# First layer norm of a fused attention and FFN block: normalisation on ScalarE, weight and bias in the transposed eviction and on GpSimd

## The reference, cut to what matters

```python
xn = layernorm(x)                                # no weight, no bias
# branch 1: attention block on xn
attn = softmax(scores(xn)) @ v                   # 16 heads of 16, causal, 512 x 512 scores a head
y = xn + (ctx @ out_w + out_b)
h = (y - mean(y)) / sqrt(var(y) + 1e-5) * ln1_g + ln1_b     # the first layer norm
f = gelu(h @ ffn_w1 + ffn_b1) @ ffn_w2 + ffn_b2             # 256 -> 1024 -> 256
s = layernorm(h + f) * ln2_g + ln2_b
# branch 2: gated FFN on xn with blockwise FP4 rounding of activations and weights
g = silu(ffn_ref(xn))                            # 256 -> 2 x 704 -> 256
out = x + s * g
```

## Time and profile before

| | us |
|---|---|
| median of 3 runs | 1925.8 (1923.6 to 1926.86) |
| the profiled execution, its own time | 1926.66 |
| its span, first to last instruction | 1924.9 |
| TensorE matmul busy | 1821.6 (95%) |
| VectorE busy | 1597.8 (83%) |
| GpSimd busy | 1165.4 (61%) |
| ScalarE busy | 950.6 (49%) |

### The profile page before, as it was taken

One profiled execution on the slowest core, in us unless ns is written; L12 is line 12 of the kernel. 1 busy time (PEld: TensorE's weight loads), 2 busy tenths in 40 slices (PEclk: granted clock), 3 DMA queues, 4 the chain that ended last, 5 costly groups with the idle time before them and its releaser, 6 DMA issues.

```text
span 1924.9 us, 37358 instructions
## 1 busy us (share of the span) xinstructions
PE 1821.6 (95%) x12693; PEld 1308.1 (68%) x12693; DVE 1597.8 (83%) x5143; ACT 950.6 (49%) x1940; POOL 1165.4 (61%) x825
## 2 busy tenths in 40 slices
PE   8886999999999999999999999999999999999997
PEld 3333667676776767677776767677776767777766
DVE  5888878888898978888897988888897888889763
ACT  3543545453635545463645545463554545364542
POOL 1434856575765757575775757586675657576472
PEclk8988999999999999999999999999999999999999
DMA  5532233333323333332323333331433333332211
GB/s 151 161 105 79 75 97 109 87 108 87 101 63 108 109 97 92 96 116 64 113 75 97 109 101 94 97 107 53 122 90 97 110 86 109 83 98 71 64 56 34
DMA packets 146647, 181.44 MB, mean 94 GB/s; under 512 B 20461, under 2 KB 101486, under 8 KB 146452
## 3 DMA queue, kind: packets, MB, share of 16 engines
...
...
## 4 chain that ended last, share of the span: by engine, by line
PE 67%; DVE 18%; issue 7%; POOL 3%; ACT 2%; DMA 2%; SPq 0%; POOLq 0%; ACTq 0%; DVEq 0%
PE ps L765 12%; PE ps L774 11%; PE ps L706 10%; PE ps L723 5%; PE ps L629 4%; PE ps L679 4%; PE ps L663 3%; PE ps L616 3%; PE ps L738 3%; PE ps L599 3%; PE ps L659 2%; DVE Pr L1072 2%; DVE nmax L1042 2%; PE ps L716 2%; POOL slot L1226 1%
## 5 line engine op out<-in xcount | busy, mean ns | idle before, releaser
L1181 POOL TENSOR_TENSOR Pr<-Pr,Tz 128x768 f32<-128x768 f32 (+2 forms) x384 | 483.2, 1288 | 141.1 <-ACT Pr L838 140.6
L1042 DVE CUSTOM_DVE_ANT_0 ps<-ps,future 128x512 f32<-128x512 f32 (+3 forms) x1024 | 478.3, 514 | 40.3 <-issue 39.5
L838 ACT ACTIVATE Pr<-ps 128x384 f32<-128x384 f32 x512 | 245.7, 490 | 297.0 <-PE ps L663 292.3
L629 PE MATMUL ps<-KS,QS 108*128 108x512 bf16 (+3 forms) x1024 | 228.6, 302 | 28.8 <-DVE nmax L1042 25.8
L765 PE MATMUL ps<-catT,w 128*128 128x256 f32 x1024 | 241.8, 382 | 0.7 <-ACT catT L901 0.7
L774 PE MATMUL ps<-w,gT 128*128 128x256 f32 x1024 | 232.2, 380 | 0.9 <-ACT gT L918 0.9
L1072 DVE SCALAR_TENSOR_TENSOR Pr<-ps,Tz 128x512 f32<-128x512 f32 x256 | 175.9, 687 | 43.3 <-ACT ps L827 42.4
L774 PEld LDWEIGHTS ps<-w,gT 128*128 128x128 f32 x1024 | 191.2, 190 | 25.2 <-ACT gT L918 1.3
L765 PEld LDWEIGHTS ps<-catT,w 128*128 128x128 f32 x1024 | 188.9, 190 | 26.9 <-issue 3.2
L1226 POOL TENSOR_TENSOR slot<-slot 128x704 f32<-128x704 f32 x64 | 107.5, 1679 | 159.9 <-DVE slot L946 159.9
L827 ACT ACTIVATE ps<-ps 128x512 f32<-128x512 f32 x256 | 151.3, 591 | 77.1 <-PE ps L659 76.8
...
## 6 DMA issues: line engine op xcount, KB each, us to landing
Tz<-kernel_rows SPq DMA_DIRECT2D x256, 256.0 KB, 3.6
...
```

The costliest lines, as they stand in the source:

```text
L629: ins = mm(o, QS[0:KROWS, 2 * p + e, it * P:(it + 1) * P], KS[0:KROWS, p, 0:n], start=True, stop=True)
L838: inc(af(Pr[:, p % 4, e, at:at + wd], src[:, 0:wd], ACT.Exp), "a_exp")
L1042: ins = v.tensor_tensor_reduce(o, o, future[:, S - n:S], -1.0, 3e38, ALU.add, ALU.min, nmax[:, 2 * pl + e, it:it + 1])
L1181: ins = g.tensor_tensor(a, a, Tz[:, p % 2, :, P * j:P * j + PAST[j]], ALU.mult)
```

## The change

The first layer norm is split anew over three engines.

- VectorE keeps the statistics. Its `lnc1` becomes one instruction of 128 x 4: shift1 = -mean * rstd. Its step `lnb1` is gone.
- ScalarE gets a step `lnb1`: four activations (Identity, scale = rstd, bias = shift1, both one value a partition) write the normalised y back to `hY`, without weight and bias.
- After the transpose a feature lies on a partition, so ScalarE's `hT` eviction applies ln1_g and ln1_b as per-partition scale and bias (`ln1_cols`, a new table of 128 x 2 x 2 that is loaded once). In the tail the eviction becomes two instructions for one.
- For the residual GpSimd multiplies `hY` by ln1_g (one more 128 x 1024 operation a batch) and adds a row that holds ffn_b2 + ln1_b, summed once in the first batch.
- The semaphore `a_h` (ScalarE's normalisation) takes the place of half of `v_h`.
- All five lists are laid out anew, in all three parts.

```diff
@@ scalar_steps, hT in the tail
-                    inc(af(catT[:, :, hf * n:(hf + 1) * n], bank(c_plan, s).rearrange("p (c n) -> p c n", c=KD), ACT.Copy),
-                        "a_hT")
+                    src = bank(c_plan, s).rearrange("p (c n) -> p c n", c=KD)
+                    for c in range(KD):
+                        ins = af(catT[:, c, hf * n:(hf + 1) * n], src[:, c, :], ACT.Identity, scale=ln1_cols[:, 0, c:c + 1],
+                                 bias=ln1_cols[:, 1, c:c + 1])
+                    inc(ins, "a_hT")
@@ scalar_steps, hT, and the new step
-                        inc(af(catT[:, c, :], bank(c_plan, s + (c,)), ACT.Copy), "a_hT")
+                        inc(af(catT[:, c, :], bank(c_plan, s + (c,)), ACT.Identity, scale=ln1_cols[:, 0, c:c + 1],
+                               bias=ln1_cols[:, 1, c:c + 1]), "a_hT")
+                elif k == "lnb1":
+                    i, ts = (s[1], range(2 * s[1], 2 * s[1] + 2)) if which == "tail" else (0, range(T))
+                    E["v_c"].wait(act, b - 1, i)
+                    for t in ts:
+                        ins = af(hY[:, t, :], hY[:, t, :], ACT.Identity, scale=rstd[:, t:t + 1], bias=shift1[:, t:t + 1])
+                    inc(ins, "a_h")
@@ vector_steps
                 elif k == "lnc1":
-                    layernorm_center(hY, row["ln1_g"], 0, s)
-                elif k == "lnb1":
-                    layernorm_finish(hY, row["ln1_b"], 0, s)
+                    n, ts = tokens_of(0, s)
+                    tt = slice(ts[0], ts[-1] + 1)
+                    E["g_rstd"].wait(dve, b - 1, n)
+                    E["a_h"].wait(dve, b - 2)
+                    inc(v.scalar_tensor_tensor(shift1[:, tt], mv[:, tt, 0], -1.0, rstd[:, tt], ALU.mult, ALU.mult), "v_c")
@@ gpsimd_steps
+                        g.tensor_tensor(row["ffn_b2"][:], row["ffn_b2"][:], row["ln1_b"][:], ALU.add).then_inc(L["row_sum"], 1)
+                        pool.wait_ge(L["row_sum"], 1)
...
-                    E["v_h"].wait(pool, b - 1, hf)
+                    E["a_h"].wait(pool, b - 1, hf)
                     d_out.wait(pool, b - 2)
-                    bias = row["ffn_b2"][:].unsqueeze(1).to_broadcast([P, tt.stop - tt.start, D])
-                    inc(g.tensor_tensor(y2[:, tt, :], hY[:, tt, :], bias, ALU.add), "g_hb2")
+                    wide = lambda n: row[n][:].unsqueeze(1).to_broadcast([P, tt.stop - tt.start, D])
+                    inc(g.tensor_tensor(y2[:, tt, :], hY[:, tt, :], wide("ln1_g"), ALU.mult), "g_hg")
+                    E["g_hg"].wait(pool, b - 1, hf)
+                    inc(g.tensor_tensor(y2[:, tt, :], y2[:, tt, :], wide("ffn_b2"), ALU.add), "g_hb2")
@@ ORDER, mid, the start of three lists
-            out.0 out.1 ln1 muld.0.0 lnc1 silu.0.0 lnb1 muld.0.1 silu.0.1 mx.1.0.0 mx.1.0.1 mx.1.0.2 muld.1.0 mx.1.0.3
+            silu.0.0 muld.0.0 out.0 out.1 ln1 muld.0.1 lnc1 silu.0.1 mx.1.0.0 mx.1.0.1 muld.1.0 mx.1.0.2 mx.1.0.3
...
-            cT out.0 out.1 sc.0.0 gu.0.0 sc.0.1 gu.0.1 sc.0.2 mx.1.0.0 mx.1.0.1 sc.0.3 sc.0.4 gu.1.0 sc.0.5 sc.1.0
+            cT gu.0.0 sc.0.0 out.0 sc.0.1 out.1 sc.0.2 sc.0.3 sc.0.4 gu.0.1 sc.0.5 sc.1.0 mx.1.0.0 mx.1.0.1 gu.1.0
...
-            cT sc.0.0 silu.0.0 sc.0.1 silu.0.1 sc.0.2 sc.0.3 sc.0.4 vcopy sc.0.5 sc.1.0 silu.1.0 sc.1.1 hT sc.1.2 sc.1.3
+            cT silu.0.0 sc.0.0 sc.0.1 sc.0.2 vcopy sc.0.3 sc.0.4 silu.0.1 sc.0.5 lnb1 sc.1.0 silu.1.0 sc.1.1 hT sc.1.2
```

More of the change, by code:

```diff
@@ L164 @@
         sync="""
-            T.0 load.1 T.1 xt T.2 xload T.3 mio.1 T.4 splitio T.5 load.0 T.6 T.7 fin mio.0
+            T.0 load.1 T.1 xt T.2 T.3 xload mio.1 T.4 T.5 splitio load.0 T.6 T.7 fin mio.0
         """,
         gpsimd="""
-            ln1 mul.0 lnb1 xnb mul.1 hq.0 xt mul.2 hr.0 hq.1 projm.0 projm.1 mul.3 projm.2 hr.1 xq mul.4 hq.2 hr.2 mul.5
+            ln1 mul.0 lnb1 xnb mul.1 hq.0 xt mul.2 hr.0 mul.3 hq.1 projm.0 projm.1 projm.2 hr.1 xq mul.4 hq.2 hr.2 mul.5
             xr ln2 fin mul.6 hq.3 mul.7 hr.3
@@ L208 @@
         gpsimd="""
-            last:ln1 last:mul.0 last:hq.0 last:hr.0 last:lnb1 last:mul.1 last:hq.1 last:mul.2 last:hr.1 last:mul.3
-            last:xnb last:hq.2 last:hr.2 last:mul.4 last:mul.5 last:hq.3 last:hr.3 last:mul.6 last:mul.7 last:ln2
-            last:fin tail:ln1.0 tail:lnb1.0 tail:ln1.1 tail:ln2.0 tail:fin.0 tail:lnb1.1 tail:ln2.1 tail:fin.1
+            last:ln1 last:mul.0 last:lnb1 last:hq.0 last:hr.0 last:mul.1 last:xnb last:hq.1 last:mul.2 last:hr.1
+            last:mul.3 last:hq.2 last:hr.2 last:mul.4 last:mul.5 last:hq.3 last:hr.3 last:mul.6 last:mul.7 last:ln2
@@ L212 @@
+            last:fin tail:ln1.0 tail:ln1.1 tail:lnb1.0 tail:ln2.0 tail:lnb1.1 tail:fin.0 tail:ln2.1 tail:fin.1
         """,
         vector="""
-            last:silu.0.0 last:out.0 last:muld.0.0 last:out.1 last:ln1 last:lnc1 last:muld.0.1 last:lnb1 last:silu.0.1
-            last:mx.1.0.0 last:silu.1.0 last:mx.1.0.1 last:muld.1.0 last:hq.0 last:mx.1.0.2 last:muld.1.1 last:silu.1.1
-            last:hr.0 last:mx.1.0.3 last:mx.1.0.4 last:mx.1.1.0 last:mx.1.1.1 last:muld.2.0 last:mx.1.1.2 last:mx.1.1.3
@@ L222 @@
-            last:ln2 last:lnc2 last:ctxt.2 last:dn.2 last:lnb2 last:ctxt.3 tail:out.0 tail:ln1.0 tail:lnc1.0 tail:lnb1.0
-            tail:out.1 tail:ln1.1 last:dn.3 tail:lnc1.1 tail:lnb1.1 tail:f2.0 tail:f2.1 tail:ln2.0 tail:lnc2.0
-            tail:lnb2.0 tail:f2.2 tail:f2.3 tail:ln2.1 tail:lnc2.1 tail:lnb2.1
+            last:silu.0.0 last:out.0 last:muld.0.0 last:out.1 last:ln1 last:silu.0.1 last:muld.0.1 last:lnc1
+            last:mx.1.0.0 last:silu.1.0 last:mx.1.0.1 last:muld.1.0 last:hq.0 last:muld.1.1 last:mx.1.0.2 last:silu.1.1
@@ L225 @@
+            last:hq.3 last:muld.6.0 last:hr.3 last:muld.6.1 last:f2.3 last:ctxt.1 last:muld.7.0 last:muld.7.1 last:dn.1
+            last:ln2 last:dn.2 last:lnc2 last:lnb2 last:ctxt.2 last:ctxt.3 tail:out.0 tail:ln1.0 tail:lnc1.0 tail:out.1
+            tail:ln1.1 last:dn.3 tail:lnc1.1 tail:f2.0 tail:f2.1 tail:ln2.0 tail:lnc2.0 tail:f2.2 tail:lnb2.0 tail:f2.3
+            tail:ln2.1 tail:lnc2.1 tail:lnb2.1
         """,
@@ L255 @@
+            tail:f1.1.2 tail:f1.1.3
         """,
@@ L1245, in gpsimd_steps @@
                     x = xn if which == "tail" else hY
-                    E["v_h"].wait(pool, b - 1, 2 + hf if which == "tail" else 1)
+                    E["v_h"].wait(pool, b - 1, hf if which == "tail" else 0)
                     E["a_gs"].wait(pool, b - 1)
```

272 lines of the change are left out of this document (138 added, 134 removed).

## The result

The changed kernel took 1899.76 us in the median of four runs (1899.45 to 1904.26), the kernel before 1925.47 us beside it (1923.6 to 1926.86). The ratio is 0.9873, 95% interval 0.9857 to 0.9888. A second set of runs of the same kernel gave 1904.06 us and 0.9885 (0.987 to 0.9899). The forecast was 1905.

What follows compares the result with a forecast made beforehand. TensorE was taken to bound a `mid` turn, 106.07 of 109.40 us busy. 14 x (0.9 + 0.6) = 21.0, less 0.4 in the tail, is 20.6: profiled 1926.66 to 1906.1, median 1905 us; range 1887 to 1924.

Steps and rivals of the forecast that it cites:

- its four microseconds: Head: TensorE's 43 us of idle time could go either way by some 4 us; change put at 0.
- The walk: Start of a `mid` turn, followed step by step: 1.3 us of waits for 2.2, gain 0.9 us a turn.
- the four small waits: New TensorE waits at a turn's start: `sc.0.4` 0.45, `sc.0.5` 0.2, `mx.1.0.4` 0.15, `mx.1.1.0` 0.5 us.
- The 0.17 that I added for each gap: TensorE gaps in a turn: each costs 0.17 us beyond its idle time, hidden in a modelled end.
- The end of the turn: Earlier `f2.3` lets VectorE's 3.16 us saving count there: 0.6 us a turn of 2.5, bounds 0 and 2.5.
- The rule that spoke against it: GpSimd shares SBUF interfaces with VectorE; one long L931-like VectorE instruction a turn would cost 1.2 us.
- GpSimd's pass: Added 128 x 1024 operation, 2.36 us a turn, fits into idle time at no cost; 2.4 if `mul.0` stays put.
- The tail: After the last turn: longer chain to `f1` costs 0.4 us, first half of tokens only; bounds 0 and 1.2.
- B: VectorE's saved time comes back as waiting for TensorE's order; 0.4 us a turn left, 1920.6 us; 15%.
- C: Start of a turn: ScalarE's normalisation makes `hT` wait, beyond 1.0 us of slack; slower, 1940 us; 9%.
- D: Nearly all TensorE idle time in the turns goes, 14 x 3.2 = 44.8 us, giving 1881 us; 12%.
- E: VectorE contention with GpSimd takes 1.2 of the 1.5 us gained a turn, giving 1922 us; 6%.

## Why the prediction was right, step by step

**The total.** -20.6 was forecast between the profiled executions, -22.4 measured. The turns gave 22.1 for 21.0. A head of -2.7, inside its four microseconds, made up for a tail that I had too small. That is luck: the head comes in two lengths (last section), and in seven profiles of variants with the changed head list it ends at 241.8 to 243.0 us, 7 to 8 us ahead of before's 250.08 (one profile) and outside the four. The median of 1899.76 lies 5 us below the forecast of 1905, and the early head may be why.

**The start of the turn.** The walk held. GpSimd's power starts 10.1 us into the turn (forecast 10.4), the activations end at 13.6 (13.6 to 13.8), TensorE reaches `hT` at 14.6 (14.8), with 0.96 us of slack (1.0); the doubled normalisation confirms that. Of the four small waits two came, 0.36 and 0.37 for 0.45 and 0.5. TensorE's idle time up to 809.00 is 0.73 us. The 0.17 that I added for each gap was too much: a turn has three gaps fewer and 1.54 us less idle time, and became 1.68 shorter, so a gap hid some 0.05 (and 0.13 by the doubled normalisation, whose turn has two gaps and 1.69 us of idle time more and is 1.95 longer). By the 0.05 the start gives 0.94 + 0.05 = 1.0 for the 0.9 forecast.

**The end of the turn.** The size was near (0.65 us of idle time and two gaps less, for 0.6), the reason was wrong, so that the size is luck. The step that failed is the claim that VectorE's saved 3.16 us are cashed there. The split with the old lists leaves all five gaps; the old computation with the new lists has only the three. The gaps go by the order. Which of the moves at the end of the turn takes away the two gaps wasn't tried: a later `f2.3` leaves the three as they are. Its early place is needed by the new lists in the middle of the turn, as filler under VectorE's rounding and so that the statistics don't meet GpSimd, and missing it costs 4.6 to 4.8 us in the ordinary turns.

**What VectorE's saving is for.** It isn't added to the gain of the lists. Lists alone +62 us, split alone +50, both -21 to -26. The new lists run GpSimd's multiplication where VectorE used to normalise. With the normalisation on ScalarE that place is free. Each of the two single parts was tried with one place of `lnb1` only, so that neither can pay at another place isn't shown.

**The rule that spoke against it.** I gave contention 6%, as a rise of small VectorE instructions. Here is what it does: two groups of four take 3.25 and 3.02 us beside GpSimd, 1.67 each without. The Trainium skill, "GPSIMD Engine Reference", section "Key points", says that VectorE and GpSimd contend for their SBUF interfaces, and the runs agree. The change takes VectorE's large groups out of its way, which I hadn't seen, and still pays a little: the pair of small instructions L1068 and L1070 in the middle of a turn takes 1.34 us or more in each turn of the changed kernel, beside GpSimd's multiplication, where the kernel before has 0.56. This costs TensorE nothing in most turns and some 0.5 us in others (last section).

**GpSimd's pass** costs nothing, as forecast, and for the reason given: `mul.0` moved up by 3.4 us (3 forecast). Where it doesn't move, the forecast price of 2.4 is measured, 2.17 and a slower clock behind it.

**ScalarE.** The four activations take 2.07 us, 0.52 apart, above my bound of 2.0. The `hT` evictions take 1.45 for two, where two copies took 1.08: 0.18 each, above 0.14. I had scaled from rows with one operand of one value a partition, and these have two. The slack swallowed it. Busy times a turn: VectorE 91.05 (91 forecast), ScalarE 55.67 (55.4), GpSimd 73.61 (72.8).

**The tail** is the mis-sized term: +0.4 with an upper bound of 1.2, measured +1.6, and +0.8 in `last`, for which I had nothing. TensorE in the tail of the changed kernel:

```profile
1863.16 3.72 PE L768 MATMUL ps<-catT,w 128*128 128x256 f32 x16 [1.11 <-ACT catT L906]
1871.49 1.99 PE L768 MATMUL ps<-catT,w 128*128 128x256 f32 x8 [0.53 <-ACT catT L906]
```

The first wait was 0.69 before, and the one before `out` is 0.74 for 0.52. The second is new: I had said that the second half has other matmuls ahead of it, and left out that ScalarE has a table load, gelus and the copy `gscopy` ahead of that eviction. The three together are 1.2 of the 1.6. The tail with `hT.1` moved up is 0.8 us shorter. The 0.8 in `last` wasn't tried; it was 0.2 in the second profile (95.38).

**The rivals.** B's mechanism, saved time coming back as waiting, is what the split alone shows at the end of the turn, where VectorE waits 0.40 for `f2.3` as before. C's place and slack were right, its price too low: a late `hT` also makes the next maximum wait. D is refuted: 1.78 us a turn stay idle, at the same places in most variants. E didn't come as forecast: VectorE's busy time fell by 3.17 us a turn, and L944 and L954 are no longer than their lines before (280 and 527 ns in the median, for 343 and 527); the pair that is held is another.
